# Two Swin blocks on one core: q and k as three fp32r products, and new orders on every engine

## The reference: what is computed

```
h = LN(x) * g1 + b1, rolled by (-3, -3), cut into windows of 7 x 7 = 49 tokens
q, k, v = h @ qkv_w + qkv_b                        # 96 -> 3 x 96
a = softmax(q * hd**-0.5 @ k.T + rel_bias + mask)  # per window and head, 49 x 49
x = x + roll_back(a @ v @ proj_w + proj_b)
m = gelu(LN(x) * g2 + b2 @ fc1_w + fc1_b)          # 96 -> 384
L0: m = LN(m) * g3 + b3
x = x + m @ fc2_w + fc2_b
```

## Time and profile before

| what | value |
|---|---|
| median of 3 runs | 6845.63 us (6843.1 to 6854.27) |
| profiled execution | 6848.46 us, its span 6846.5 us |
| PE busy, share of the span | 6637.3 us, 97% |
| ACT | 5460.3 us, 80% |
| DVE | 5211.6 us, 76% |
| POOL | 4494.8 us, 66% |
| DMA, mean | 48 GB/s |
| mean granted clock of TensorE | 0.993 |

### The profile page before, as it was taken

One profiled execution on the slowest core, in us unless ns is written; L12 is line 12 of the kernel. 1 busy time (PEld: TensorE's weight loads), 2 busy tenths in 40 slices (PEclk: granted clock), 3 DMA queues, 4 the chain that ended last, 5 costly groups with the idle time before them and its releaser, 6 DMA issues.

```text
span 6846.5 us, 283694 instructions
## 1 busy us (share of the span) xinstructions
PE 6637.3 (97%) x97324; PEld 5821.8 (85%) x97324; DVE 5211.6 (76%) x18725; ACT 5460.3 (80%) x11268; POOL 4494.8 (66%) x4612
## 2 busy tenths in 40 slices
PE   6999999999999999999999999999999999999998
PEld 5888888888888888888888888888888888888887
DVE  5777777777777777777777777777777777777775
ACT  4888888888888888888888888888888888888886
POOL 3666666666666666666666666666666666666664
PEclk8999999999999999999999999999999999999998
DMA  2111111111111111111111111111111111111111
GB/s 63 47 50 45 50 46 49 47 49 47 49 48 48 48 47 48 47 49 47 50 46 50 46 50 45 50 45 50 46 50 47 49 47 49 47 48 48 48 48 34
DMA packets 604527, 327.79 MB, mean 48 GB/s; under 512 B 449916, under 2 KB 603902, under 8 KB 604094
## 3 DMA queue, kind: packets, MB, share of 16 engines
q1 hardware_dynamic: 603992, 322.32, 18.2%
q10 hardware_dynamic: 486, 4.82, 0.2%
HBM read 82.89 MB, written 38.54 MB: 18 GB/s over the span
## 4 chain that ended last, share of the span: by engine, by line
PE 44%; SPq 39%; DMA 8%; issue 6%; ACT 2%; DVE 1%; POOL 0%; POOLq 0%; DVEq 0%; ACTq 0%
SPq L343 20%; PE ps L396 13%; SPq L331 10%; PE ps L486 10%; DMA vM<-vA 8%; PE ps L422 6%; PE ps L453 3%; SPq L321 3%; PE ps L510 3%; PE ps L432 3%; PE ps L414 3%; ACT kT L641 2%; SPq L313 2%; PE ps L523 2%; SPq L300 2%
## 5 line engine op out<-in xcount | busy, mean ns | idle before, releaser
L975 POOL TENSOR_TENSOR hid_sq<-hid 128x1176 f32<-128x1176 f32 x256 | 550.1, 2149 | 1443.2 <-ACT hid L696 1443.2
L679 ACT ACTIVATE probsT<-ps 98x392 f32<-98x392 f32 x2048 | 952.9, 492 | 498.9 <-PE ps L396 498.4
L848 DVE TENSOR_TENSOR shifted<-ps,negmax 113x392 f32<-113x392 f32 x2048 | 1161.3, 567 | 213.2 <-DVE negmax L844 0.5
L844 DVE TENSOR_REDUCE negmax<-ps 113x8 f32<-113x392 f32 x2048 | 1147.3, 560 | 208.8 <-PE ps L453 208.5
L396 PE MATMUL ps<-ident,probs 113*98 113x113 f32 x8192 | 1076.5, 264 | 9.5 <-ACT probs L672 5.8
L486 PE MATMUL ps<-vM,probsT 98*49 98x18 f32 (+1 forms) x32768 | 944.5, 202 | 134.1 <-DMA vM<-vA 132.4
L486 PEld LDWEIGHTS ps<-vM,probsT 98*49 98x49 f32 x32768 | 838.4, 125 | 272.6 <-issue 163.6
L672 ACT ACTIVATE probs<-shifted 113x392 f32<-113x392 f32 x2048 | 988.5, 518 | 9.8 <-DVE shifted L848 6.8
L664 ACT ACTIVATE ps<-table 113x392 f32 (+1 forms) x2048 | 956.4, 498 | 13.9 <-DVE y_out L880 2.6
L396 PEld LDWEIGHTS ps<-ident,probs 113*98 113x98 f32 x8192 | 801.0, 128 | 129.6 <-issue 81.1
L947 POOL TENSOR_TENSOR rstdA<-var_epsA,minus_half 98x4 f32<-98x4 f32 x512 | 517.4, 1011 | 576.5 <-DVE var_epsA L827 576.3
(11 more groups left out here) (98 smaller groups left out, 14713.8 us busy)
## 6 DMA issues: line engine op xcount, KB each, us to landing
kM<-kT SPq DMA_DIRECT2D x512, 85.8 KB
vM<-vA SPq DMA_DIRECT2D x1024, 41.3 KB
vM<-vA SPq DMA_DIRECT2D x1024, 38.3 KB
x_in<-in_x SPq DMA_DIRECT2D x256, 147.0 KB
x_again<-in_x SPq DMA_DIRECT2D x256, 147.0 KB
kM<-kT SPq DMA_DIRECT2D x1024, 36.8 KB
x_keep<-x_next SPq DMA_DIRECT2D x256, 147.0 KB
out_y<-y_out SPq DMA_DIRECT2D x256, 147.0 KB
```

Source lines behind the costliest of these rows:

```text
L679: act.activation(probsT[:, unit_buffer(L, u), :, :, :], free(ps[bank_of[f"T{L}{u}"]][0:PT, 0:1], (SP, 4), (64, 2), (1, TOK)), ACT.Copy).th ...
L844: dve.tensor_reduce(negmax[:, buf, :], s, AX.X, ALU.max, negate=True).then_inc(s_mx[L], 1)
L848: dve.tensor_tensor(shifted[0:SP, buf, :].rearrange("p (h k) -> p h k", k=TOK), s, free(negmax[:, buf, 0:1], (1, 8), (0, TOK)), ALU.add).t ...
```

## The change

LAST goes from 5 to 6. Four things change.

1. q and k of both blocks are made of three fp32r products of high and low parts, by a helper `three` that fc1 now uses too. ACT makes xqT_high as a further copy in `turned`; DVE makes xqT_low (`low_part_qk`); the setup makes wqk_high and wqk_low (NW goes from 21 to 27). v still uses the float32 xnT.
2. The waiting product at the scores of L0 is replaced by an increment of a semaphore `s_ready`, which nobody waits for.
3. The bodies of all five engines are in a new order, over strips s0 to s6.
4. The ring of banks is new, and the bank of xtA is free after s_ql (the low part) instead of s_xe.

```diff
+            def three(out, w_high, w_low, x_high, x_low, low_ready):
+                pe.matmul(out, w_high, x_high, start=True, stop=False)
+                pe.matmul(out, w_low, x_high, start=False, stop=False)
+                pe.wait_ge(*low_ready)
+                return pe.matmul(out, w_high, x_low, start=False, stop=True)
             def q(x, L):
...
-                    pe.matmul(ps[bank_of[f"q{L}"]][0:QK[L], 0:ST], wqkv[L][:, 0:QK[L]], xnT[L][:, :], start=True, stop=True)\
-                      .then_inc(s_q[L], 1)
+                    three(ps[bank_of[f"q{L}"]][0:QK[L], 0:ST], wqk_high[L][:, 0:QK[L]], wqk_low[L][:, 0:QK[L]],
+                          xqT_high[L][:, :], xqT_low[L][:, :], (s_ql[L], x.count(1, 1))).then_inc(s_q[L], 1)
...
-                    pe.matmul(ps[bank_of["sc00"]][0:1, 0:1], ident[:, 1:2], ident[:, 0:1], start=False, stop=True, skip_group_check=True)
+                    pe.sem_inc(s_ready, 1)
...
+                    act.activation(xqT_high[L][0:C, :], g, ACT.Copy).then_inc(s_xh[L], 1)
                     act.activation(xnT[L][0:C, :], g, ACT.Copy).then_inc(s_xe[n], 1)
...
+            def low_part_qk(x, L):
+                if x.exists(ns):
+                    dve.wait_ge(s_xe[f"A{L}"], x.count(1, 1))
+                    if x.back().exists(ns):
+                        dve.wait_ge(s_q[L], x.back().count(1, 1))
+                        dve.wait_ge(s_k[L], x.back().count(1, 1))
+                    dve.tensor_tensor(xqT_low[L][0:C, :], ps[bank_of[f"xtA{L}"]][0:C, 0:ST], xqT_high[L][0:C, :].bitcast(f32),
+                                      ALU.subtract).then_inc(s_ql[L], 1)
```

More of the change, by code:

```diff
@@ L346, in body @@
             def body(i):
-                s0, s1, s2, s3, s5 = Strip(i, 0), Strip(i, 1), Strip(i, 2), Strip(i, 3), Strip(i, 5)
+                s0, s2, s4, s6 = Strip(i, 0), Strip(i, 2), Strip(i, 4), Strip(i, 6)
+                variants(s2, 0)
                 load(s0)
[L349 to L355, removed]
+                load_residual(s2)
+                variants(s4, 1)
+                spread_v(s2, 0)
+                store(s6)
+                keep(s4)
+                spread_v(s4, 1)
             iterate(sp, body)
@@ L519, in fc1 @@
                         pe.wait_ge(*free_from)
-                    g = ps[bank_of[use]]
                     w = slice(128 * c, 128 * (c + 1))
[L523 to L527, removed]
+                    three(ps[bank_of[use]][:, 0:ST], wfc1_high[L][:, w], wfc1_low[L][:, w], xnT_high[L][:, :], xnT_low[L][:, :],
+                          (s_xl[L], x.count(1, 1))).then_inc(s_f1[L], 1)
             def fc2(x, L):
@@ L556, in body @@
             def body(i):
[L557 to L598, removed]
+                s1, s2, s3, s4, s5, s6 = Strip(i, 1), Strip(i, 2), Strip(i, 3), Strip(i, 4), Strip(i, 5), Strip(i, 6)
@@ new lines, in body @@
+                v(s2, 0)
+                probs_turn(s5, 1, 2)
+                k(s2, 0)
+                probs_turn(s5, 1, 3)
+                o_turn(s3, 0)
+                q(s2, 0)
+                xT(s6, "M1")
+                project(s3, 0)
+                attend(s5, 1, 0)
+                attend(s5, 1, 1)
+                attend(s5, 1, 2)
+                probs_turn(s5, 1, 4)
+                probs_turn(s5, 1, 5)
+                xT(s4, "A1")
+                scores(s2, 0, (0, 1))
+                attend(s5, 1, 3)
@@ new lines, in body @@
+                attend(s5, 1, 4)
+                attend(s5, 1, 5)
+                fc1(s6, 1, 0)
+                xT(s1, "A0")
+                q(s4, 1)
+                xT(s3, "M0")
+                k(s4, 1)
+                fc1(s6, 1, 1)
+                o_turn(s5, 1)
+                fc1(s6, 1, 2)
+                fc1(s3, 0, 0)
+                fc1(s3, 0, 1)
+                fc1(s3, 0, 2)
+                project(s5, 1)
+                fc2(s6, 1)
+                scores(s4, 1, (0, 1, 2))
+                v(s4, 1)
@@ L600, in _ @@
+                probs_turn(s2, 0, 0)
+                fc2(s3, 0)
+                probs_turn(s2, 0, 1)
+                scores(s4, 1, (3, 4, 5))
+                attend(s2, 0, 0)
+                attend(s2, 0, 1)
+                probs_turn(s4, 1, 0)
+                probs_turn(s4, 1, 1)
             iterate(pe, body)
@@ new lines, in body @@
+                exps(s5, 1, 2)
+                probsT_out(s5, 1, 0)
+                probsT_out(s5, 1, 1)
+                exps(s5, 1, 3)
+                v_out(s2, 0)
+                probsT_out(s5, 1, 2)
+                k_out(s2, 0)
+                probsT_out(s5, 1, 3)
+                o_out(s3, 0)
+                q_out(s2, 0)
+                exps(s5, 1, 4)
+                turned(s6, "M1")
+                exps(s5, 1, 5)
+                seed(s2, 0, 0)
+                seed(s2, 0, 1)
+                probsT_out(s5, 1, 4)
@@ new lines, in body @@
+                probsT_out(s5, 1, 5)
+                turned(s4, "A1")
+                gelu(s6, 1, 0)
+                turned(s1, "A0")
+                turned(s3, "M0")
+                k_out(s4, 1)
+                q_out(s4, 1)
+                o_out(s5, 1)
+                gelu(s6, 1, 1)
+                gelu(s6, 1, 2)
+                gelu(s3, 0, 0)
+                gelu(s3, 0, 1)
+                gelu(s3, 0, 2)
+                seed(s4, 1, 0)
+                seed(s4, 1, 1)
+                seed(s4, 1, 2)
@@ L744, in _ @@
+                exps(s2, 0, 0)
+                v_out(s4, 1)
+                seed(s4, 1, 3)
+                seed(s4, 1, 4)
+                probsT_out(s2, 0, 0)
+                exps(s2, 0, 1)
+                seed(s4, 1, 5)
+                exps(s4, 1, 0)
+                exps(s4, 1, 1)
+                probsT_out(s2, 0, 1)
             iterate(act, body)
```

108 lines of the change are left out of this document (55 added, 53 removed), and 12 rows, old and new, of the table BANKS.

## The result

The changed kernel takes 6769.1 us (median of 4 runs, 6768.22 to 6771.77), the kernel before, beside it, 6844.4 us (6842.89 to 6854.27). The ratio is 0.9886 with a 95% interval of 0.9874 to 0.9898. It is faster, but by 75 us where 204 were forecast: inside the range, and at the size of rival 2.

The account below looks back on a forecast made before the run. PE, 97% busy, bounded the kernel, with a recurring wait for a DMA; DVE would set the new period. 166 + 255 x 25.4 = 6643 us of span, corrected to 6642 us, 3.0% faster; range 6555 to 6785 us.

Parts of the forecast that it names:

- rival 2: A new wait in the loop takes most of what the old one gave: period 25.7 to 26.2 us, chance 0.18.
- the walk: Tracing the new engine lists with old durations to find what is late next: DVE sets the period, 25.4 us.
- DVE's circle: Closed chain from fc2 on PE through DVE and ACT back to PE: 25.11 us, 0.34 over PE's floor.
- Rival 1: PE's floor is reached, hand-overs free and DVE a little shorter: period 24.8 to 25.1 us, 6528 us, chance 0.11.
- Rivals 3 and 4: DVE's circle grows: 7000 us, chance 0.06; weight loads don't hide behind the three products: 6992 us, chance 0.03.
- Rival 5: The three products for q and k save nothing; counted inside the main forecast, with no chance of its own.
- Floor: PE's work per strip in the new order, the least the period can be: 24.77 us, down from 25.72.
- The waiting product: PE's product waiting ahead of the scores of L0: removing it gains 0.12 us a strip, bounds +0.12 to -0.11.
- The neighbours: Unchanged PE operations get shorter beside other operations in the new order: 0.55 us a strip, bounds 0 to 0.7.
- SP's circle: Old closed chain PE, ACT, SP, DMA, PE, with 0.53 us of PE waiting for vM; the new order opens it.
- The hand-overs: Late hand-overs at three tight places on DVE's circle, up to 0.23 us each; one to two taken, 0.3 us.
- Filling and draining: Time outside the 255 periods, setup included: 155.3 us before plus 8.6 and 2.2, 166 us, bounds 155 to 185.

Follow-up runs that it names:

- e1: The changed kernel with gelu's wait for fc2 of the strip before put ahead of its wait for fc1: 6504.8 us.
- e2: The kernel before, with a semaphore increment between gelu's two waits so that the table load starts only after fc1: 7187.9 us.
- e7: e1 with q and k as one float32 product each again, without the added ACT copies and DVE subtractions: 6582.4 us.
- e4: e1 with the waiting product put back ahead of the scores of L0 in place of the semaphore increment: 6532.6 us.
- e6: e3 with one more wait, so that POOL's squares start only after DVE's var_epsM: 7126.2 us.
- e3: The kernel before with only q and k changed to three fp32r products, with their copies and subtractions; old order and banks kept: 7168.5 us.

## Why the prediction failed in size

**The step that failed** is the walk, "I walked through the new lists with the distances of the old timelines". It has no term for the table load in front of gelu(s6, 1, 0), since at the old distances that load is hidden behind fc1. The walk gave P = 25.4 with DVE setting it. Measured is 25.97, and ACT sets it through one load of 1.28 us that can't run ahead. Neither the lists of operations nor the code of `gelu`, which is the same in both kernels, show this; the order of instructions in the loop does. e1, which changes nothing but the order of the two waits, takes 264 us back, and e2, with the load held, makes the other kernel 344 us slower (DVE's meeting with POOL included).

**Which case came.** Rival 2 in its size (P 25.7 to 26.2, 6770 us), and in its form: a new wait takes most of what the old one gave. Its place was named wrongly (turned or kM, on DVE's circle), so that the time lies inside the stated range is luck. Rival 1 was true of the order itself: with the load free, P is 24.85 and no circle binds. Rivals 3 and 4 didn't come. Rival 5, that the three products save nothing, falls with e7.

**PE's list.** Floor 24.77 forecast, 24.85 measured in e1. q and k: 0.28 us a strip forecast, 0.30 in e7. A group 0.61 forecast, 0.60 measured. The waiting product: 0.12 forecast, 0.11 in e4. The neighbours then gave 26.25 - 0.53 - 0.30 - 0.11 - 24.85 = 0.46 us, against 0.55: worked out from the others, not measured alone.

**Weight loads.** PE's load rows of the changed kernel stand 0.17 to 0.18 us apart, each beginning inside the product before, in the same 97 rows of the array:

```profile
3402.24 0.17 PEld L418 LDWEIGHTS ps<-xqT_high,wqk_low 97*96 97x96 f32 x1
3402.41 0.16 PEld L420 LDWEIGHTS ps<-xqT_low,wqk_high 97*96 97x96 f32 x1
```

Rival 4 is refuted. The sentence of the Trainium skill ("TensorE: Matmul & The Clock Gate", Part 3) on which it leaned, that loads overlap with products in flight only when the row group differs, doesn't hold for this shape. The same Part also lets a load into the background weight buffer be pulled ahead; the rows can't tell whether it is that.

**SP's circle** opened as forecast: no wait for vM<-vA recurs in the loop of the changed kernel. In e6, in the old order, it is there with 0.89 us.

**DVE's circle**, 25.11 us, didn't bind; in e1 the period is 0.26 under it, which the prediction itself named as the sign that the DVE row is too long. One term was mis-sized: third_stats 1.57 us, of which the changed kernel takes 0.76 (3415.76 to 3416.52). With that the circle comes to 25.11 - 0.81 = 24.30 us, less than PE's list of 24.77. So DVE as what sets P was the second thing the walk had wrong.

```profile
3415.76 0.17 DVE L914 COPY st<-ps 98x8 f32<-98x8 f32 x1 [0.39 <-PE ps L560]
3415.96 0.16 DVE L918 SCALAR_TENSOR_TENSOR var<-st 98x4 f32<-98x4 f32 x1
3416.16 0.16 DVE L921 TENSOR_TENSOR var<-var,st 98x4 f32<-98x4 f32 x1
3416.35 0.17 DVE L923 TENSOR_SCALAR var<-var 98x4 f32<-98x4 f32 x1
3417.03 0.57 DVE L870 TENSOR_REDUCE negmax<-ps 113x8 f32<-113x392 f32 x1 [0.51 <-PE ps L466]
```

The old row held one of these operations at 0.92 us, and beside it an operation of POOL; DVE's row and then POOL's, of the kernel before:

```profile
3423.63 0.92 DVE L895 TENSOR_TENSOR var<-var,st 98x4 f32<-98x4 f32 x1
```

```profile
3423.53 1.00 POOL L966 TENSOR_TENSOR x_biased<-x_mid,bfc 98x384 f32<-98x384 f32 x1
```

Both end within 0.02 us of each other. That was a property of the old order, and the walk carried it over. The last line of the changed kernel's shows DVE waiting for PE at the place where I had it run without a gap. The hand-overs, 0.3 us, cost next to nothing: 24.85 - 24.77 leaves 0.08 for all of them.

**Filling and draining.** Forecast 166 us. e1 has 6502.1 - 255 x 24.85 = 165 to 166. The changed kernel has 145, because its unrolled iterations are 1 to 1.2 us shorter than its P; this shows too that the rest can't be read apart from the loop. With P of e1 the sum of the prediction would have been 166 + 255 x 24.85 + 2 - 3 = 6502 us, 3 from what was measured. That closeness is in part luck: e1's unrolled iterations hold the load, for which the forecast had no term. From the seventh last of its gelu loads to the last are 157.9 us, in the changed kernel 144.5, so some 13 us of e1's rest, by this estimate, come from there.

## What to carry to other kernels

A table load of ACT hides only if no wait stands ahead of it that ends late. Where an operation that needs another table has two waits, the order in the code doesn't settle which of them stands ahead of the load: the late wait had to come last in the changed loop, and first in the old loop and in all unrolled iterations. Only the list of instructions shows it, and it has to be read again after every change of lags or order, for the loop and the unrolled part apart. When an order is planned from old durations, look at each short operation whose duration is far over that of its like, since it met another engine there and needn't again. Before a new order is judged by its time, look for a wait that the loop has and the unrolled iterations lack, or the other way round: here it hid 264 of 340 us.

## What the runs showed of the hardware

**A load runs ahead up to the wait in front of it.** 1.28 us of ACT_TABLE_LOAD were free in the loops of before and e1, where the load started ahead of its input, and cost 1.12 us of the period where it waited for fc1 (after against e1). ACTIVATE follows 1.29 us after the load's start when it is ready (3402.16 to 3403.45). The Trainium skill, "ScalarE: Activation LUTs", section "What ACT_TABLE_LOAD costs", gives some 1283 ns for the load, with which the rows agree, and 1380 ns more for a drain, of which these rows show nothing.

**Small DVE operations beside POOL.** Operations on 98x4 values in SBUF that started behind a POOL operation lasted to its end: 0.92 instead of 0.16 us, 2.15 instead of 0.17. The one that started 0.03 us ahead (before, 3416.50) took its 0.17 us. Nor is it always so behind one: in the changed kernel two of 0.16 us lie beside a root on 98x4 values on POOL (3415.30, 1.02 us) and aren't stretched. The Trainium skill, "Advanced Engine Details and Errata", section "GPSIMD Details", says that POOL shares a read and a write interface with DVE, with conflicts where the DVE instruction is in a 2-port perf mode or has two SBUF inputs. The stretched rows agree with a shared interface. The conditions don't tell the rows apart: var<-var,st, with two SBUF inputs, is stretched in the kernel before and not in the changed one.

**Idle spells and the clock.** Behind waits of 0.37 and 0.59 us the granted clock stood at 0.51 for 3.5 us in one of sixteen periods of e3, which added 1.6 us to that period; in the others it stayed at 1.00 behind the same waits. Behind 0.89 and 0.34 us it fell in one of three periods of e6. In the changed kernel one wait of 0.81 us in each period left it at 1.00 over the middle 5000 us. So an order with more and scattered waits can cost more than their sum, but what decides in which period the clock falls isn't shown.
